# First stage of a two-stage kernel: PE's small products behind convolution products, weights of two images mixed one phase later, norms applied by ScalarE

## Chip, cores and metric

The kernel runs on one core of a Trainium2 chip. The metric is the device time of one execution in microseconds (us), the median of several runs.

## What is computed

A batch of 32 images of 32x32 pixels and 64 channels passes two residual layers, each behind a group norm (32 groups of two channels). The first one is what this case is about:

```python
for t in range(3):                                   # STEPS
    k, v = x @ Wk, x @ Wv                            # two heads of 16
    attn = softmax(q . k / 4 over the 1024 pixels)
    logits = pooled(attn, v) @ Wmlp                  # one number for each of 4 experts
    weights = softmax(where(allowed, logits, -1e9) / 1.5)
    wsel = the two largest weights, normalized to sum 1
    x_mod = x * (1 + mean_over_heads(attn) * 1024 * softplus(alpha))
    x = sum over e of wsel[e] * (conv3x3(x_mod, We[e]) + be[e])
    allowed loses the top expert of this step (never the last one)
x_out = x_in + x                                     # then the second group norm
```

The second layer is two Mamba scans, over rows and over columns. The change does not touch it.

## The kernel before

`stage1` (L243) computes the first layer and both group norms, `stage2` (L873) the scans. Stage 1 keeps an image as 128 partitions (two row parities x 64 channels) by 512 pixels. Four images are a team, two teams a body, four bodies the batch. For each body there are six phases k = 0 to 5: step k // 2 of team g = k % 2. So while the vector work of a phase decides on the weights of one team, TensorE runs the convolution of the other team, which is the phase before (`last` in `slot`, L511). The convolution is not done four times, once for each expert: VectorE mixes the four experts' weights with `wsel` first (`mix_first`, `mix_second`, `mix_last`, L821 to L836; ScalarE's `scale_experts` makes the first term), and TensorE multiplies once, by six fp32 products of 128x512 for each image: three on the padded image (`conv_main`, L495) and three on a copy shifted by a row (`conv_anti`, L504, the copy is ScalarE's `shift`).

Each engine has an order written out by hand, its `slot`, and meets the others by counting semaphores; nothing is scheduled by a program. For phase P the chain between the engines is: `score` (PE, L459, four products into `p_route`) -> `reduce_max` (DVE, L736) -> `swap` (PE, L465) -> `neg_top` (DVE, L743) -> `exp` (ACT, L596) -> the weighted sum `parts` (DVE, L755) -> `total` (PE, L469) -> `r`, `ratio`, `ratios`, `kmap`, `mod_w` (DVE, L760 to L765) -> `logits` (PE, L473) and `modulation` (PE, L479) -> the choice of experts, `wsel` (DVE, L782 to L811) with ScalarE's `prob` in it -> `scale_experts` and the mixes. `modulate` (DVE, L776) writes the padded image. ScalarE's `step_out` (L570) moves a finished convolution to `xc`, from which `score` of the next step of that team reads; in the last step DVE's `step_last` (L701) adds it to `x1` instead.

Group norms are laid into some phases (`norm_in_phase`, L371): the input norm of team 0 in k = 5 and of team 1 in k = 0, the norm of the result of team 0 in k = 1 and of team 1 in k = 2. That makes 4 of 6 phases of a body "norm phases" (in the first body only k = 0). Each has `norm_moments` (DVE, L652, four `bn_stats`), two tiny products on PE (`group_mean` L441, `group_var` L446), `norm_variance_in`, `norm_variance`, ScalarE's Ln and Exp (`group_root`) and `norm_apply` (DVE, L674), whose last increment (`x_norm` or `x_out`) lets `score` or the stores of the SP queue go on. A hardware loop (`each_phase`, L358) runs k = 5 of a body with k = 0 to 4 of the next, three times.

Of the kernel before, what the change touches and what calls it, by code (L numbers as in the profile page):

```python
# [24 lines left out]
PHASES = 2 * STEPS  # L25
# [222 lines left out]
def stage1(nc, x_in, mid_x, norm_rows, c):  # L248
# [10 lines left out]
    with ctx:  # L259
# [61 lines left out]
        gn_rs = sem("s1_gn_rs")  # L321
        x_norm = sem("s1_x_norm")
# [115 lines left out]
        def _(pe):  # L438
# [69 lines left out]
            def slot(i, k, before, after):  # L508
                norm = norm_in_phase(i, k, before, after)
                P = i * PHASES + k  # L510
                last = (i, k - 1) if k else (i - 1, PHASES - 1)  # L511
                runs_conv = k > 0 or before
                if runs_conv:
                    conv_main(*last, 0)
                score(i, k, TEAM - 1)
                swap(P)
                if norm:
                    group_mean(norm[0])
                if runs_conv:
                    conv_anti(*last, 0)  # L520
                total(P)
                if norm:
                    group_var(norm[0])
                if runs_conv:
                    conv_main(*last, 1)
                logits(P)
                modulation(P, 0)
                modulation(P, 1)
                if runs_conv:
                    conv_anti(*last, 1)  # L530
                    conv_main(*last, 2)
                modulation(P, 2)
                if runs_conv:
                    conv_anti(*last, 2)
                modulation(P, 3)
                if runs_conv:
                    conv_main(*last, 3)
                    conv_anti(*last, 3)
                if after:
                    for a in range(TEAM - 1):  # L540
                        score(*((i, k + 1) if k < PHASES - 1 else (i + 1, 0)), a)
# [17 lines left out]
        def _(act):  # L559
            def group_root(n):  # L560

                act.wait_ge(gn_v, n + 1)
                nc.scalar.activation(gn[:, 4, :], gn[:, 3, :], ACT.Ln).then_inc(gn_ln, 1)
                act.wait_ge(gn_ln, n + 1)
                nc.scalar.activation(gn[:, 5, :], gn[:, 4, :], ACT.Exp, scale=-0.5).then_inc(gn_rs, 1)

# [53 lines left out]
            group_root(0)  # L620
            act.wait_ge(zeroed, ZEROS)
            each_phase(act, slot)
            group_root(4 * BODIES - 2)
            group_root(4 * BODIES - 1)

# [10 lines left out]
        def _(dve):  # L636
# [25 lines left out]
            def norm_variance_in(n):  # L662

                dve.wait_ge(gn_mean, n + 1)
                chain(nc.vector.tensor_copy(gn[:, 0, :], p_gn[:, P_MEAN]))
# [8 lines left out]
            def norm_apply(n, src, dst, finish):  # L674
# [7 lines left out]
                for a in team:  # L682
                    to = dst[a][:] if finish is x_norm else dst[a][:, :, PAD:]
                    x = src[a][:] if finish is x_norm else src[a][:].rearrange("p (j w) -> p j w", w=SIDE)
# [4 lines left out]
            def group_norm(n, src, dst, finish):  # L689
                norm_moments(src)  # L690
                norm_variance_in(n)
                norm_variance(n)
                norm_apply(n, src, dst, finish)
# [13 lines left out]

            def slot(i, k, before, after):
                g, t = k % 2, k // 2
                P = i * PHASES + k  # L710
                if k == PHASES - 1 and not isinstance(i, int):
# [8 lines left out]
                if norm:  # L720
                    number, kind, pair = norm
                    body = i + 1 if k == PHASES - 1 else i
                    src, dst, finish = ((fresh[pair], xc[pair], x_norm) if kind == "in" else
                                        (x1[pair], xn[pair], x_out))
# [26 lines left out]
                if norm:  # L751
                    norm_variance_in(number)
# [15 lines left out]
                if norm:  # L768
                    norm_variance(number)
# [50 lines left out]

                def mix_first(a):  # L821
                    dve.wait_ge(scaled, 4 * P + a + 1)
                    nc.vector.scalar_tensor_tensor(mix0[a % 2][:], c["we"][:, 1, :], wsel[:, a, 1:2], mix0[a % 2][:],  # L823
                                                   ALU.mult, ALU.add).then_inc(mix_ready, 1)

                def mix_second(a):
                    dve.wait_ge(mix_ready, 8 * P + (1, 2, 5, 6)[a])
                    nc.vector.scalar_tensor_tensor(mix0[a % 2][:], c["we"][:, 2, :], wsel[:, a, 2:3], mix0[a % 2][:],
                                                   ALU.mult, ALU.add).then_inc(mix_ready, 1)

                def mix_last(a):
                    dve.wait_ge(mix_ready, 8 * P + (3, 4, 7, 8)[a])

                    ge(dve, conv_done, 4 * (P - 2) + a + 1)
                    nc.vector.scalar_tensor_tensor(w_mixed[g][a][:].rearrange("p m d c -> p (m d c)"), c["we"][:, 3, :],
                                                   wsel[:, a, 3:4], mix0[a % 2][:], ALU.mult, ALU.add).then_inc(w_ready, 1)  # L836
# [16 lines left out]
                if norm and kind == "out":  # L853
                    norm_apply(number, src, dst, finish)
# [9 lines left out]
            group_norm(0, fresh[0], xc[0], x_norm)  # L864
            each_phase(dve, slot)
            x1_last = (BODIES - 1, 1)
            group_norm(4 * BODIES - 2, x1[0], xn[0], x_out)
            step_last(*x1_last, team)
            x1_complete(*x1_last)
            group_norm(4 * BODIES - 1, x1[1], xn[1], x_out)  # L870
# [637 lines left out]
```

## Time and profile before

| | us |
|---|---|
| median of 3 runs | 4278.47 (4276.27 to 4280.89) |
| the profiled execution, its own time | 4277.8 |
| its span in the trace | 4275.8 |
| busy in the span: PE | 3856.6 (90%) |
| DVE | 3902.4 (91%) |
| ACT | 2860.6 (67%) |
| POOL | 3142.5 (73%) |

Stage 1 runs from 31.6 to 932 us of the span, stage 2 from there to the end. PE's granted clock over the whole execution has a mean of 0.952 of full speed. A "busy" PE may still run at half clock, and "idle before" is the time that an engine stood in front of an instruction, with what ended it.

### The profile page before, as it was taken

The numbers are of one execution on the slowest core, as the hardware profiler recorded it, in microseconds if no ns is written. First come the engines' busy times: TensorE is split into PE (matmuls) and PEld (weight loads), VectorE is DVE, ScalarE is ACT, GpSimd is POOL, SyncE is SP. The second block draws the span as 40 slices with busy tenths as digits, with TensorE's granted clock in tenths as the row PEclk, the third lists the DMA queues.
The fourth block names the chain that finished last, engine by engine and source line by source line (L and its number), as shares of the span: only waits on it lengthen the run. The fifth ranks groups of instructions, "written<-read, shape, count | busy, mean of one in ns | idle before, by whom it ended". The sixth has DMA issues, their size and how long they took to land. (4 is left out here: it accounts for less than half of the span.)

```text
span 4275.8 us, 49280 instructions
## 1 busy us (share of the span) xinstructions
PE 3856.6 (90%) x8924; PEld 1606.4 (38%) x8924; DVE 3902.4 (91%) x5354; ACT 2860.6 (67%) x4337; POOL 3142.5 (73%) x1446
## 2 busy tenths in 40 slices
PE   4988988869999999999999999999999999999998
PEld 2333333323333333333333333333333333333433
DVE  5676767659999999999999999999999999999998
ACT  2323232327777777777777777777777777777775
POOL 0000000009999999999999999999999999999998
PEclk8999999989999999999999999999999999999999
DMA  2001010128888888888888888888888888888886
GB/s 74 0 23 59 20 61 0 61 104 350 330 342 342 345 328 340 345 331 337 328 345 342 344 342 325 337 339 349 341 320 348 343 338 329 329 342 345 349 337 256
DMA packets 199056, 1156.59 MB, mean 270 GB/s; under 512 B 30001, under 2 KB 30801, under 8 KB 67665
## 3 DMA queue, kind: packets, MB, share of 16 engines
q1 hardware_dynamic: 198736, 1153.31, 68.9%
q14 instruction: 239, 1.95, 0.1%
q8 instruction: 81, 1.33, 0.1%
HBM read 1118.87 MB, written 34.34 MB: 270 GB/s over the span
## 5 line engine op out<-in xcount | busy, mean ns | idle before, releaser
L1362 POOL TENSOR_TENSOR read<-state,bc_all 128x1024 f32<-128x1024 f32 x1024 | 2401.8, 2362 | 182.2 <-DVE state L1420 170.7
L1420 DVE TENSOR_TENSOR_SCAN state<-decays,p_drive 128x512 f32<-128x512 f32 x2048 | 2430.1, 1207 | 38.3 <-ACT decays L1297 18.4
L1148 PE MATMUL p_y<-read,ident 128*128 128x512 f32 x4096 | 1998.7, 622 | 26.1 <-issue 17.1
L1297 ACT ACTIVATE decays<-dt,wa 128x496 f32<-128x496 f32 x2048 | 1322.3, 698 | 19.3 <-issue 16.9
L1148 PEld LDWEIGHTS p_y<-read,ident 128*128 128x128 f32 x4096 | 793.1, 198 | 1064.7 <-issue 950.7
L1409 DVE TENSOR_TENSOR p_drive<-bc_all,p_dtx 128x512 f32<-128x512 f32 x1536 | 1037.5, 675 | 0.0
L1369 POOL TENSOR_TENSOR dtx<-dt,xconv 128x512 f32<-128x512 f32 x128 | 163.5, 1278 | 916.5 <-ACT dt L1244 916.5
L1379 POOL TENSOR_TENSOR pool_drive<-dtx,bc_all 128x1024 f32<-128x1024 f32 x256 | 603.8, 2359 | 0.9 <-DMA bc_all<-bc_scratch 0.9
L1305 ACT COPY p_drive<-pool_drive 128x1024 f32<-128x1024 f32 x256 | 259.7, 1014 | 325.2 <-POOL pool_drive L1379 325.2
L1144 PE MATMUL p_y<-xconv,d_diag 128*128 128x512 f32 x256 | 161.7, 716 | 207.9 <-DVE gated L1428 207.9
L504 PE MATMUL p_conv<-shf,wm 128*128 128x512 f32 x576 | 303.9, 669 | 0.0
L1244 ACT COPY dt<-p_b 128x512 f32<-128x512 f32 x128 | 75.0, 586 | 303.7 <-PE p_b L1139 303.7
L495 PE MATMUL p_conv<-pad,wm 128*128 128x512 f32 x576 | 269.9, 605 | 0.0
L570 ACT ACTIVATE xc<-p_conv,bias 128x512 f32<-128x512 f32 x64 | 44.0, 687 | 210.9 <-PE p_conv L504 210.9
L1223 ACT ACT_TABLE_LOAD x128 | 164.2, 1283 | 22.8 <-PE p_a L1096 20.5
L823 DVE SCALAR_TENSOR_TENSOR mix<-we_sb,wsel,mix 128x768 f32<-128x768 f32 x96 | 94.9, 1016 | 91.2 <-ACT mix L577 91.0
L504 PEld LDWEIGHTS p_conv<-shf,wm 128*128 128x128 f32 x576 | 115.7, 211 | 156.6 <-issue 152.0
L1232 ACT ACT_TABLE_LOAD x128 | 164.2, 1283 | 2.3
L1102 PE MATMUL p_a<-cols_in,w_cols 128*128 128x256 f32 x640 | 157.2, 394 | 3.9 <-ACT cols_in L1290 3.9
L1144 PEld LDWEIGHTS p_y<-xconv,d_diag 128*128 128x128 f32 x256 | 39.8, 195 | 314.1 <-DVE gated L1428 313.0
L495 PEld LDWEIGHTS p_conv<-pad,wm 128*128 128x128 f32 x576 | 106.3, 191 | 134.5 <-issue 121.6
L1124 PE MATMUL p_a<-xconv,wbc 128*32 128x512 f32 x256 | 134.7, 608 | 15.3 <-ACT xconv L1223 14.8
(164 smaller groups left out, 3316.5 us busy)
## 6 DMA issues: line engine op xcount, KB each, us to landing
bc_all<-bc_scratch SPq DMA_DIRECT2D x1024, 1024.0 KB, 7.2
norm_rows<-xn SPq DMA_DIRECT2D x32, 280.0 KB, 2.8
norm_in<-norm_rows SPq DMA_DIRECT2D x64, 140.0 KB, 6.0
norm_in<-norm_rows SPq DMA_DIRECT2D x64, 139.8 KB, 7.1
fresh<-in_x SPq DMA_DIRECT2D x32, 256.0 KB, 3.3
x<-in_x SPq DMA_DIRECT2D x32, 256.0 KB, 3.5
mid_x<-x SPq DMA_DIRECT2D x32, 256.0 KB, 2.6
resid<-mid_x SPq DMA_DIRECT2D x32, 256.0 KB, 7.6
```

The source lines that it names most:

```text
L495: nc.tensor.matmul(bank[:], w_mixed[g][a][:, 0, dx, :], padded[g][a][:, :, dx:dx + SIDE], start=(dx == 0), stop=False)
L504: mm = nc.tensor.matmul(bank[:], w_mixed[g][a][:, 1, dx, :], shifted[g][a][:, :, dx:dx + SIDE], start=False, stop=(dx == 2))
L1144: nc.tensor.matmul(p_y[:], d_diag[unit[0]][:], xconv[b][:], start=True, stop=False).then_inc(skip_added, 1)
L1148: nc.tensor.matmul(p_y[:], ident[:], read[:, s % DEEP, :], start=False, stop=(s == N - 1)).then_inc(y_added, 1)
L1223: nc.scalar.activation(same_shape(xconv[b][:], m), in_order(p_a, m), ACT.Silu, bias=wcb[m][:]).then_inc(xconv_ready, 1)
L1232: nc.scalar.preload_act_table_set("natural_log_exp_and_others")
L1297: nc.scalar.activation(decays[s % DEEP][:].rearrange("p (q t) -> p q t", t=SIDE)[:, :, 1:], dt[b][:, :, 1:], ACT.Exp, scale=wa[m][:, s:s + ...
L1305: nc.scalar.copy(p_drive[:, s % 4:s % 4 + 2, :], pool_drive[n][:]).then_inc(drive_moved, 1)
L1362: nc.gpsimd.tensor_tensor(read[:, s % DEEP:s % DEEP + 2, :], state[:, s % DEEP:s % DEEP + 2, :], bc_all[:, s:s + 2, 1, :], ALU.mult).then_ ...
L1379: nc.gpsimd.tensor_tensor(pool_drive[n][:], dtx[b][:].unsqueeze(1).broadcast_to([128, 2, PIX]), bc_all[:, s:s + 2, 0, :], ALU.mult).then_i ...
L1409: nc.vector.tensor_tensor(p_drive[:, s % 4, :], bc_all[:, s, 0, :], p_dtx[:], ALU.mult).then_inc(drive_done, 1)
L1420: nc.vector.tensor_tensor_scan(state[:, s % DEEP, :], decays[s % DEEP][:], p_drive[:, s % 4, :], 0.0, ALU.mult, ALU.add).then_inc(scan_don ...
```

## The change

1. PE's `slot`: `swap` (and `group_mean`) now stand behind `conv_anti(last, 0)`, `total` and `group_var` behind `conv_main(last, 1)`, and `logits` and the first two modulations behind `conv_anti(last, 1)`; the later ones are shifted by half an image likewise.
2. DVE: of images 2 and 3 the six mixes are no longer done at the end of their own phase but in the next one (`late`): two behind `reduce_max`, two behind `parts`, one behind `ratios` (and `norm_variance`), one behind `mod_w`. For the last phase of all they stand in front of the closing norms.
3. DVE: `norm_moments` stands in front of `reduce_max` instead of behind it.
4. `norm_apply` moves from DVE to ScalarE (four `activation` with scale and bias for each norm). DVE computes the bias -mean x rstd by one more small instruction (`norm_scale`), earlier than before: in front of the mixes of images 0 and 1. DVE waits (`free`) until the norm before has been applied before it overwrites `gn`.
5. ScalarE: `group_root` in front of `prob`; `norm_apply` behind `scale_experts` 0 and 1; both shifts of images 0 and 1 in front of `scale_experts` 2 and 3.

The diff, cut:

```diff
@@ PE slot
                 score(i, k, TEAM - 1)
+                if runs_conv:
+                    conv_anti(*last, 0)
                 swap(P)
                 if norm:
                     group_mean(norm[0])
                 if runs_conv:
-                    conv_anti(*last, 0)
+                    conv_main(*last, 1)
                 total(P)
                 if norm:
                     group_var(norm[0])
                 if runs_conv:
-                    conv_main(*last, 1)
+                    conv_anti(*last, 1)
                 logits(P)
                 modulation(P, 0)
                 modulation(P, 1)
                 if runs_conv:
-                    conv_anti(*last, 1)
                     conv_main(*last, 2)
+                    conv_anti(*last, 2)
                 modulation(P, 2)
                 if runs_conv:
-                    conv_anti(*last, 2)
+                    conv_main(*last, 3)
                 modulation(P, 3)
                 if runs_conv:
-                    conv_main(*last, 3)
                     conv_anti(*last, 3)
@@ ScalarE
+            def norm_apply(n, kind, pair):
+                act.wait_ge(gn_scale, n + 1)
+                for a in team:
+                    src, dst = ((fresh[pair][a][:], xc[pair][a][:]) if kind == "in" else
+                                (x1[pair][a][:].rearrange("p (j w) -> p j w", w=SIDE), xn[pair][a][:, :, PAD:]))
+                    o = nc.scalar.activation(dst, src, ACT.Identity, scale=gn[:, 9, a:a + 1], bias=gn[:, 7, a:a + 1])
+                o.then_inc(x_norm if kind == "in" else x_out, 1)
@@ ScalarE slot
+                if norm:
+                    group_root(norm[0])
                 act.wait_ge(wexp_in, P + 1)
                 nc.scalar.activation(prob[:], logit[:], ACT.Exp, scale=1.0 / 1.5).then_inc(wexp_done, 1)
-                if norm:
-                    group_root(norm[0])
...
                 scale_experts(P, 0)
                 scale_experts(P, 1)
+                if norm:
+                    norm_apply(*norm)
                 if steps:
                     step_out(i, k - 1, 2)
                 shift(P, g, 0)
+                shift(P, g, 1)
                 scale_experts(P, 2)
-                shift(P, g, 1)
+                scale_experts(P, 3)
                 if steps:
                     step_out(i, k - 1, 3)
-                scale_experts(P, 3)
                 shift(P, g, 2)
                 shift(P, g, 3)
@@ DVE: norm_apply becomes norm_scale
-                for a in team:
...
-                    o = nc.vector.tensor_scalar(to, x, gn[:, 0, a:a + 1], gn[:, 9, a:a + 1],
-                                                ALU.subtract, ALU.mult)
-                o.then_inc(finish, 1)
+                nc.vector.scalar_tensor_tensor(gn[:, 7, :], gn[:, 0, :], -1.0, gn[:, 9, :],
+                                               ALU.mult, ALU.mult).then_inc(gn_scale, 1)
@@ DVE slot
+                def late(stage, *images):
+
+                    if runs_conv:
+                        for a in images:
+                            stage(P - 1, 1 - g, a)
...
+                    free = {5: (x_out, 2 * i), 0: (x_norm, 2 * i + 1), 1: (x_norm, 2 * i + 2), 2: (x_out, 2 * i - 1)}[k]
...
-                dve.wait_ge(score_done, P + 1)
-                nc.vector.reduce_max(top[0:R, :], p_route[0:R, :], X).then_inc(top_ready, 1)
                 if norm:
                     if kind == "in":
                         dve.wait_ge(fresh_in[pair], 16 * TEAM * body + 16 * TEAM)
                     norm_moments(src)
+                dve.wait_ge(score_done, P + 1)
+                nc.vector.reduce_max(top[0:R, :], p_route[0:R, :], X).then_inc(top_ready, 1)
+                late(mix_first, 2, 3)
...
+                late(mix_second, 2, 3)
                 dve.wait_ge(sum_done, P + 1)
...
+                if norm:
+                    norm_variance(number)
+                late(mix_last, 2)
                 chain(nc.vector.tensor_scalar(kmap[:], r[:], float(PIX), c["gain"][0:R, 3:4], ALU.mult, ALU.mult))
...
-                if norm:
-                    norm_variance(number)
+                late(mix_last, 3)
...
+                if norm:
+                    norm_scale(number)
                 for stage in (mix_first, mix_second, mix_last):
                     for a in (0, 1):
-                        stage(a)
+                        stage(P, g, a)
                 modulate(2)
-                if norm and kind == "in":
-
-                    norm_apply(number, src, dst, finish)
                 modulate(3)
-                for stage in (mix_first, mix_second, mix_last):
-                    for a in (2, 3):
-                        stage(a)
@@ DVE, behind the last phase
             each_phase(dve, slot)
             x1_last = (BODIES - 1, 1)
+            for stage in (mix_first, mix_second, mix_last):
+                for a in (2, 3):
+                    stage(PHASES * BODIES - 1, 1, a)
```

How the order moves. First TensorE, from `score` of image 3 of a phase without a norm (k = 2 of the first body) to its third modulation. Before:

```order
L459 MATMUL p_route<-xc,route 128x512
L465 MATMUL p_small<-top,neg_swap 128x1
L504 MATMUL p_conv<-shf,wm 128x512 x3
L469 MATMUL p_small<-parts,both_par 128x2
L495 MATMUL p_conv<-pad,wm 128x512 x3
L473 MATMUL p_small<-ratios,ones 128x16
L479 MATMUL p_modul<-attn,mod_w 128x512 x2
L504 MATMUL p_conv<-shf,wm 128x512 x3
L495 MATMUL p_conv<-pad,wm 128x512 x3
L479 MATMUL p_modul<-attn,mod_w 128x512
```

The same stretch after the change:

```order
L460 MATMUL p_route<-xc,route 128x512
L505 MATMUL p_conv<-shf,wm 128x512 x3
L466 MATMUL p_small<-top,neg_swap 128x1
L496 MATMUL p_conv<-pad,wm 128x512 x3
L470 MATMUL p_small<-parts,both_par 128x2
L505 MATMUL p_conv<-shf,wm 128x512 x3
L474 MATMUL p_small<-ratios,ones 128x16
L480 MATMUL p_modul<-attn,mod_w 128x512 x2
L496 MATMUL p_conv<-pad,wm 128x512 x3
L505 MATMUL p_conv<-shf,wm 128x512 x3
```

Three convolution products stand between `score` and `swap` now, where none did; three between `swap` and `total` and three between `total` and `logits`, as before.

Then VectorE in the same phase, from `reduce_max` (`top`) to `mod_w`. Before (the six mixes of images 2 and 3 stood just ahead of this):

```order
L736 TENSOR_REDUCE top<-p_route 64x1
L743 SCALAR_TENSOR_TENSOR neg_top<-top,p_small 64x1
L748 SCALAR_TENSOR_TENSOR allowed<-rank,allowed 128x4x3
L750 TENSOR_SCALAR penalty<-allowed 128x16
L755 ISA scrap,parts<-p_route,attn 64x512
L755 ISA parts 64x1
L760 RECIPROCAL r<-p_small 64x1
L761 TENSOR_TENSOR ratio<-p_small,r 64x1
L762 TENSOR_SCALAR ratios<-pick,ratio 64x16
L763 TENSOR_SCALAR kmap<-r,gain 64x1
L765 TENSOR_SCALAR mod_w<-spread,kmap 64x512
```

After the change, from `neg_top` on (ahead of it stand `top` and, new, two mixes `mix_0` and `mix_1` of images 2 and 3):

```order
L783 SCALAR_TENSOR_TENSOR neg_top<-top,p_small 64x1
L788 SCALAR_TENSOR_TENSOR allowed<-rank,allowed 128x4x3
L790 TENSOR_SCALAR penalty<-allowed 128x16
L795 ISA scrap,parts<-p_route,attn 64x512
L795 ISA parts 64x1
L728 SCALAR_TENSOR_TENSOR mix_0<-we_sb,wsel,mix_0 128x768
L728 SCALAR_TENSOR_TENSOR mix_1<-we_sb,wsel,mix_1 128x768
L801 RECIPROCAL r<-p_small 64x1
L802 TENSOR_TENSOR ratio<-p_small,r 64x1
L803 TENSOR_SCALAR ratios<-pick,ratio 64x16
L735 SCALAR_TENSOR_TENSOR wm<-we_sb,wsel,mix_0 128x768
L807 TENSOR_SCALAR kmap<-r,gain 64x1
```

Five of the six moved mixes now stand inside the chain from `top` to `mod_w`, two of them between `parts` and `r`.

## Rows read from the trace of the kernel before

**Rows 1.** Windows: length, busy PE, PEld, DVE, ACT, POOL, then clock, DMA share, GB/s.
```profile
46.26:84.16 37.90, 23.74 (x40) 9.89 (x40) 26.23 (x74) 9.51 (x17) 0.00 (x0) 0.68 0.16 55
84.16:206.30 122.14, 118.31 (x280) 48.78 (x280) 80.03 (x184) 46.94 (x76) 0.00 (x0) 1.00 0.00 0
206.30:858.02 651.72, 578.25 (x1308) 243.24 (x1308) 454.05 (x1165) 199.72 (x342) 0.00 (x0) 0.92 0.10 37
858.02:932.26 74.24, 49.44 (x112) 21.55 (x112) 39.15 (x105) 10.04 (x19) 0.00 (x0) 0.82 0.16 60
```

**Rows 2.** The same view by phase: a plain one, k = 0, 1, 2, 3.
```profile
145.24:175.77 30.53, 29.58 (x70) 12.20 (x70) 20.00 (x47) 11.73 (x19) 0.00 (x0) 1.00 0.00 1
...
678.17:715.39 37.22, 33.16 (x74) 14.03 (x74) 28.98 (x76) 9.52 (x17) 0.00 (x0) 0.91 0.00 0
715.39:755.49 40.10, 33.31 (x74) 14.19 (x74) 26.59 (x72) 12.04 (x21) 0.00 (x0) 0.91 0.00 0
755.49:794.33 38.84, 32.26 (x74) 13.77 (x74) 26.58 (x73) 12.03 (x21) 0.00 (x0) 0.90 0.23 84
794.33:827.49 33.16, 32.20 (x70) 13.35 (x70) 20.09 (x48) 11.73 (x19) 0.00 (x0) 0.91 0.27 98
```

**Rows 3.** Timeline of PE around one plain phase's start (start, duration, engine, line).
```profile
607.79 1.02 PE L459 MATMUL p_route<-xc,route 128*128 128x512 f32 x2
...
609.76 0.38 PE L465 MATMUL p_small<-top,neg_swap 128*128 128x1 f32 x2 [0.95 <-DVE top L736]
610.01 2.82 PE L504 MATMUL p_conv<-shf,wm 128*128 128x512 f32 x6
...
612.67 0.28 PE L469 MATMUL p_small<-parts,both_par 128*128 128x2 f32 x2
612.81 2.82 PE L495 MATMUL p_conv<-pad,wm 128*128 128x512 f32 x6
...
615.56 0.39 PE L473 MATMUL p_small<-ratios,ones 64*128 64x16 f32 x2
615.80 1.96 PE L479 MATMUL p_modul<-attn,mod_w 64*128 64x512 f32 x4
```

**Rows 4.** The same timeline: DVE and ACT of that phase.
```profile
609.04 0.67 DVE L736 TENSOR_REDUCE top<-p_route 64x1 f32<-64x512 f32 x1
...
610.19 0.15 DVE L743 SCALAR_TENSOR_TENSOR neg_top<-top,p_small 64x1 f32<-64x1 f32 x1 [0.47 <-PE p_small L465]
...
611.37 0.69 DVE L755 CUSTOM_DVE_ANT_0 scrap<-p_route,attn 64x512 f32<-64x512 f32 x1 [0.74 <-ACT attn L596]
...
612.99 0.16 DVE L760 RECIPROCAL r<-p_small 64x1 f32<-64x1 f32 x1 [0.92 <-PE p_small L469]
...
613.36 0.23 DVE L762 TENSOR_SCALAR ratios<-pick,ratio 64x16 f32<-64x16 f32 x1
...
613.84 0.48 DVE L765 TENSOR_SCALAR mod_w<-spread,kmap 64x512 f32<-64x512 f32 x1
```

**Rows 5.** Timeline of a norm phase (k = 0): PE, then DVE.
```profile
681.70 0.59 PE L441 MATMUL p_gn<-moments,group_mean 128*128 128x4 f32 x2 [2.41 <-DVE moments L659]
682.15 5.47 PE L504 MATMUL p_conv<-shf,wm 128*128 128x512 f32 x6
...
678.78 2.46 DVE L654 BATCH_NORM_STATS2 stats<-fresh 128x6 f32<-128x512 f32 x4
...
704.11 0.15 DVE L678 TENSOR_TENSOR gn<-gn 128x4 f32<-128x4 f32 x1
...
705.70 1.92 DVE L685 TENSOR_SCALAR xc<-fresh,gn 128x512 f32<-128x512 f32 x4
...
708.13 1.94 DVE L823 SCALAR_TENSOR_TENSOR mix<-we_sb,wsel,mix 128x768 f32<-128x768 f32 x2
709.98 1.94 DVE L828 SCALAR_TENSOR_TENSOR mix<-we_sb,wsel,mix 128x768 f32<-128x768 f32 x2
```

**Rows 6.** Group of ScalarE's instructions, 40 to 930 us: busy, mean ns, idle before.
```profile
L570 ACT ACTIVATE xc<-p_conv,bias 128x512 f32<-128x512 f32 x64 | 44.0, 687 | 210.9 <-PE p_conv L504 210.9
```

More of the change, by code:

```diff
@@ L321, in stage1 @@
         gn_rs = sem("s1_gn_rs")
+        gn_scale = sem("s1_gn_scale")
         x_norm = sem("s1_x_norm")
@@ L620, in _ @@
             group_root(0)
+            norm_apply(0, "in", 0)
             act.wait_ge(zeroed, ZEROS)
@@ L623, in _ @@
             group_root(4 * BODIES - 2)
+            norm_apply(4 * BODIES - 2, "out", 0)
             group_root(4 * BODIES - 1)
+            norm_apply(4 * BODIES - 1, "out", 1)
         @block.gpsimd
@@ L660, in norm_moments, with norm_variance_in @@
                 ag.then_inc(gn_mean_in, 1)
-            def norm_variance_in(n):
+            def norm_variance_in(n, free=None):
                 dve.wait_ge(gn_mean, n + 1)
+                if free:
+                    ge(dve, *free)
                 chain(nc.vector.tensor_copy(gn[:, 0, :], p_gn[:, P_MEAN]))
@@ L672, in norm_variance, with norm_scale @@
                 nc.vector.tensor_scalar(gn[:, 3, :], p_gn[:, P_VAR], 1e-5, None, ALU.add).then_inc(gn_v, 1)
-            def norm_apply(n, src, dst, finish):
+            def norm_scale(n):
                 dve.wait_ge(gn_rs, n + 1)
@@ L681, in norm_apply, with group_norm @@
                     chain(nc.vector.tensor_tensor(gn[:, dst_r, :], gn[:, 6, :], gn[:, src_r, :], ALU.mult))
-                for a in team:
-                    to = dst[a][:] if finish is x_norm else dst[a][:, :, PAD:]
-                    x = src[a][:] if finish is x_norm else src[a][:].rearrange("p (j w) -> p j w", w=SIDE)
-                    o = nc.vector.tensor_scalar(to, x, gn[:, 0, a:a + 1], gn[:, 9, a:a + 1],
-                                                ALU.subtract, ALU.mult)
-                o.then_inc(finish, 1)
-            def group_norm(n, src, dst, finish):
+                nc.vector.scalar_tensor_tensor(gn[:, 7, :], gn[:, 0, :], -1.0, gn[:, 9, :],
+                                               ALU.mult, ALU.mult).then_inc(gn_scale, 1)
+            def group_norm(n, src, free=None):
                 norm_moments(src)
-                norm_variance_in(n)
+                norm_variance_in(n, free)
                 norm_variance(n)
-                norm_apply(n, src, dst, finish)
+                norm_scale(n)
             def step_last(i, g, some):
@@ L706, in x1_complete, with mix_first, mix_second, mix_last @@
                 dve.wait_ge(x1_ready, 8 * i + 4 * g + 4)
+            def mix_first(P, g, a):
+                dve.wait_ge(scaled, 4 * P + a + 1)
+                nc.vector.scalar_tensor_tensor(mix0[a % 2][:], c["we"][:, 1, :], wsel[:, a, 1:2], mix0[a % 2][:],
+                                               ALU.mult, ALU.add).then_inc(mix_ready, 1)
+            def mix_second(P, g, a):
+                dve.wait_ge(mix_ready, 8 * P + (1, 2, 5, 6)[a])
+                nc.vector.scalar_tensor_tensor(mix0[a % 2][:], c["we"][:, 2, :], wsel[:, a, 2:3], mix0[a % 2][:],
+                                               ALU.mult, ALU.add).then_inc(mix_ready, 1)
+            def mix_last(P, g, a):
+                dve.wait_ge(mix_ready, 8 * P + (3, 4, 7, 8)[a])
+                ge(dve, conv_done, 4 * (P - 2) + a + 1)
+                nc.vector.scalar_tensor_tensor(w_mixed[g][a][:].rearrange("p m d c -> p (m d c)"), c["we"][:, 3, :],
+                                               wsel[:, a, 3:4], mix0[a % 2][:], ALU.mult, ALU.add).then_inc(w_ready, 1)
             def slot(i, k, before, after):
@@ L710, in slot @@
                 P = i * PHASES + k
+                runs_conv = k > 0 or before
+                def late(stage, *images):
+                    if runs_conv:
+                        for a in images:
+                            stage(P - 1, 1 - g, a)
                 if k == PHASES - 1 and not isinstance(i, int):
@@ L722, in slot @@
                     body = i + 1 if k == PHASES - 1 else i
-                    src, dst, finish = ((fresh[pair], xc[pair], x_norm) if kind == "in" else
-                                        (x1[pair], xn[pair], x_out))
+                    src = fresh[pair] if kind == "in" else x1[pair]
+                    free = {5: (x_out, 2 * i), 0: (x_norm, 2 * i + 1), 1: (x_norm, 2 * i + 2), 2: (x_out, 2 * i - 1)}[k]
                 if k == PHASES - 1:
@@ L751, in slot @@
                 if norm:
-                    norm_variance_in(number)
+                    norm_variance_in(number, free)
                 dve.wait_ge(exp_done, P + 1)
@@ L819, in slot @@
                 chain(nc.vector.reduce_sum(bias[g][:], bias_e[:], X))
[L821 to L836, printed above, removed]
+                if norm:
+                    norm_scale(number)
                 for stage in (mix_first, mix_second, mix_last):
                     for a in (0, 1):
-                        stage(a)
+                        stage(P, g, a)
                 modulate(2)
-                if norm and kind == "in":
-                    norm_apply(number, src, dst, finish)
                 modulate(3)
-                for stage in (mix_first, mix_second, mix_last):
-                    for a in (2, 3):
-                        stage(a)
                 if ending:
@@ L852, in slot @@
                     x1_complete(*ending)
-                if norm and kind == "out":
-                    norm_apply(number, src, dst, finish)
             loop_start = [0]
@@ L863, in _ @@
             dve.wait_ge(fresh_in[0], 16 * TEAM)
-            group_norm(0, fresh[0], xc[0], x_norm)
+            group_norm(0, fresh[0])
             each_phase(dve, slot)
             x1_last = (BODIES - 1, 1)
-            group_norm(4 * BODIES - 2, x1[0], xn[0], x_out)
+            for stage in (mix_first, mix_second, mix_last):
+                for a in (2, 3):
+                    stage(PHASES * BODIES - 1, 1, a)
+            group_norm(4 * BODIES - 2, x1[0], (x_out, 2 * BODIES - 2))
             step_last(*x1_last, team)
             x1_complete(*x1_last)
-            group_norm(4 * BODIES - 1, x1[1], xn[1], x_out)
+            group_norm(4 * BODIES - 1, x1[1], (x_out, 2 * BODIES - 1))
 def stage2(nc, mid_x, norm_rows, out, c):
```

## Prediction

> **What bounds the kernel now.** I read the windows first, by stretch, and see where stage 1's time lies: the first phase takes 37.90 us (with the first `score`, which starts at 46.3), four phases without a norm 122.14, the 18 phases of the three loop turns 651.72, and the last phase with the close 74.24 [rows 1]. Stage 2 is not touched, so only these 886 of 4276 us can move, but for 932.26 us minus 46.26 nothing else runs beside them. Then the windows by phase [rows 2]. A plain phase lasts 30.53 us with PE busy 29.58 at a granted clock of 1.00: PE bounds it. Norm phases last 37.22 (k = 0), 40.10 (k = 1) and 38.84 (k = 2), with k = 5 measured like k = 0, and the clock falls to 0.91. There PE waits, and VectorE, though busy only 26.6 to 29.0 of about 38 us, is what it waits for: VectorE's 28.98 in k = 0 all lie ahead of the next `top`, but for a wait in the middle.
>
> The timeline says where PE loses time. In a plain phase it stands still 0.95 us between `score` and `swap`, since `top` must be made first; nothing is queued that could fill it [rows 3]. In a norm phase it waits 2.41 us more in front of `group_mean`, because four `bn_stats` (2.46 us) stand between `top` and the moments, and the convolution products that come next last from 682.15 to the next product at 687.41, 5.26 us instead of the 2.66 of a plain phase (610.01 to 612.67) [rows 3, 5]: TensorE runs them at 1.2 instead of 2.4 GHz after that stand. The rest is VectorE's end of the phase: six mixes, and ahead of or behind them eight small instructions (704.11 to 705.70) and four applications (1.92 us) [rows 5].
>
> **The change, part by part.** Call A the moment at which PE is through with `score` of image 3. A product is issued every 0.86 us (its row ends 0.16 later than the next one can start), so in the plain phase A = 607.79 + 0.86 = 608.65 [rows 3].
>
> *PE's floor.* A phase holds the same products before and after. A plain one without any stand takes 30.53 - 0.95 - 0.16 = 29.42 us. A norm phase has two tiny products more, 0.45 us for one on its own (681.70 to 682.15 [rows 5]) and about 0.3 in a stream like `total` and `logits` (0.14 and 0.24 [rows 3]): floor 30.0.
>
> *The chain from A to the first modulation, plain phase.* PE: `conv_anti` 0 takes 2.57, `swap` 0.25, `conv_main` 1 2.67, `total` 0.14, `conv_anti` 1 2.77, `logits` 0.24: PE could start the modulations at A + 8.64. VectorE: `top` starts at A + 0.27 (0.39 in the row, where VectorE was 0.12 late) and takes 0.61 to the next start; two late mixes at 0.93 each (1.85 for a pair [rows 5]) end at A + 2.75, which `swap` (A + 2.57) covers. `neg_top` starts 0.43 behind `swap`, at A + 3.00; `parts` starts 1.18 later (610.19 to 611.37 [rows 4]), A + 4.18, and takes 0.69. PE's `total` waits for `parts` no longer than PE is busy (A + 5.49). Now two mixes, to A + 6.73; without them `r` would have started 0.32 behind `total`, at A + 5.81, so they cost 0.9. `ratios` starts 0.37 later and takes 0.15 to the next start, A + 7.25; one mix, A + 8.18; `kmap` and `mod_w` (0.33 + 0.48 [rows 4]) end at A + 8.99. PE takes the modulations about 0.05 later, at A + 9.04: a stand of 0.4 us where PE could have gone on at 8.64. Period 29.42 + 0.4 = 29.8, against 30.53. The moved `swap` saves 1.1 us, the mixes in the chain give back 0.4.
>
> *Does VectorE reach the next `top` in time?* From `mod_w` on: one mix, `logits` 0.73, `modulate` and the choice of experts to `wsel` (about 3.4 with the first modulate), A + 13.8; `bias` and ScalarE's first terms, A + 16.3; six mixes 5.6, two modulates 1.2: A + 23.1. The next `top` is due at A + 30.1, so 7 us are free.
>
> *Norm phases.* PE runs 0.5 us later by its tiny products, VectorE 0.2 later by `norm_variance`; the four small instructions of `norm_variance_in` lie beside ScalarE's exp. So the stand nearly closes: period 30.0 to 30.1. VectorE carries `norm_scale` (nine at 0.20 = 1.8), the moments (2.8 with `bn_aggr`), in k = 5 and 0 four `step_last` (2.8) and with k = 0 and 1 behind it two memsets: 23.1 + 0.2 + 1.8 + 2.8 + 2.8 + 0.2 = A + 30.9 less the 0.4 that the sum of a plain phase waits for ScalarE and I count twice, about A + 30.5, against 30.3. On time to some tenths, and `swap` needs `top` only 2.57 behind A, so up to a microsecond is free. ScalarE: `norm_apply` starts at about A + 18.5 and takes 4 x 0.6 = 2.5 (0.687 each [rows 6], starts 0.6 apart), so `x_norm` is there at A + 21.1; the next `score` needs it at A + 24.8. In k = 1 and 2 `step_out` 2 stands behind it and is done at A + 21, needed at 26.5. ScalarE has room (9.5 to 12.0 us busy in such a phase [rows 2]). PE has no stand of microseconds left, so nothing runs at 1.2 GHz; that is worth 2.6 us in each of k = 0, 1, 2, 3, and part of k = 5.
>
> *First phase.* `x_norm` 0 comes 0.8 later, by ScalarE's slower application and one instruction. Then the moments leave the way from `top` to `neg_top` (-2.3, since `swap` still takes 0.5), six mixes and a modulate leave the way to `x_norm` 1 (-5.8 and -0.6 with what they stood behind), application and handover cost 1.0 more: 0.8 - 2.3 - 6.4 + 1.0 = -6.9.
>
> *Close.* VectorE has the six own late mixes (5.6) behind the last phase, in which it also did those of the phase before. They stood there before too, but `step_last` and the modulates now wait for PE until A + 24.8, then six mixes end at A + 30.4; before, the moments began at 885.5, 27.9 behind A. All of PE's last products wait for these: +2.5. The last application on ScalarE +1.0. Together +3.5.
>
> *Sum.* First phase -6.9; four plain phases 4 x 29.8 = 119.2 against 122.14, -2.9; 18 looped ones 3 x (4 x 30.05 + 2 x 29.8) = 539.4 against 651.72, -112.3; close +3.5. That is -118.6 against the profiled execution's 4277.8: 4159.2. Its time is 0.7 under the median of the runs, so 4160 for the median.
>
> A rule speaks against the move to ScalarE. Here an application costs 1.92 / 4 = 0.48 us on VectorE [rows 5] and 0.6 to 0.69 on ScalarE [rows 6]. The Trainium skill ("ScalarE: Activation LUTs", Rules for kernel authors) says to use VectorE and not ScalarE for multiplications and additions, and budgets some 0.3 us plus 0.83 ns per element for an activation, 0.73 us here; the trace agrees in the direction. By it each norm would take 1.0 us longer, which counts only in the first phase and the close: the sum would stand within a microsecond of mine.
>
> **Rivals.**
> (a) *VectorE's chain is longer than I count*, by semaphore latencies between the late mixes and their neighbours, 0.5 to 1.2 us a phase. For it: `mod_w` is late already in my sum, so each tenth goes straight into all 22 phases. Against: most handovers are read from rows. 22 x 0.5 to 1.2 = 11 to 26: 4171 to 4186. Chance 0.14.
> (b) *The floor is reached*: `mod_w` is in time. 4 x 0.4 + 6 x 0.4, some tenths in the norm phases, and less at the close: 4150 to 4154. Chance 0.06.
> (c) *Norm phases stay bound by VectorE*: its sum in k = 5 and 0 comes within tenths of the period. If it is 2 us longer there, six or seven phases lose 1 to 2 beyond the slack, and with k = 1 as many: 4175 to 4195. Chance 0.05.
> (d) *The rule above decides*: ScalarE waits for `norm_scale`, and `scale_experts` and `step_out` wait behind it. It decides when `x_norm` is over 3.7 us later than counted; each microsecond beyond costs one in six phases. Applications at 0.73 bring 0.5, so they don't. With 2 us beyond, 4172. Chance 0.02.
> (e) *Slower than before.* In the chain from `parts` to `mod_w` a late mix waits for an event of PE that itself stands behind the modulation, so that PE stands until VectorE is through with its queue. Nearest case: VectorE reaching `mod_w` only where it now reaches the first mixes of a phase, some 7 us later. It decides from 118.6 / 22 = 5.4 us a phase; at 7 it would be 4160 + 154 = 4314. Against: `mix_last` waits for convolutions two phases back and for its own predecessors alone. Chance 0.01.
> (f) *The change does nothing*, PE's products being issued so far ahead that order does not matter. The 0.95 us in front of `swap` in every plain phase speak against. 4278, chance 0.01.
> A slower-than-before outcome short of (e), by anything else, gets 0.01.
>
> **How the numbers follow.** My forecast, 4155 to 4168, has 0.70. The range takes in (b) and most of (a), and half of (c): 4150 to 4180. About 0.2% (8.6 us) can be told from no change: 0.97 faster, 0.01 the same, 0.02 slower.
>
> **What would show it.** The windows: plain phases of 29.8 us, norm phases of 30.0 to 30.2, clock 1.00 from the first body to the last phase. The timeline of PE: no stand in front of `swap`, `group_mean` or `total`, one of about 0.4 in front of the first modulation of a plain phase, `conv_anti` 0 in 2.6 us everywhere. VectorE idle some 7 us in front of `top` in plain phases and almost nothing in k = 0 and 1. It is wrong if PE waits for `mod_w` more than a microsecond (a), for `x_norm` (d), or for `top` (c).

## The result and the profile after

The changed kernel takes 4160.77 us (median of 4 runs, 4157.54 to 4161.57) against 4279.15: a ratio of 0.9722, 95% interval 0.9708 to 0.9737, 118 us less. Its profiled span is 4159.5 us. The forecast was 4160.

The windows of the changed kernel, cut at its own starts of `top`, the first from 46.26 as in [rows 1] (columns as there): first phase, four plain phases, 18 looped ones.

```profile
46.26:76.70 30.44, 22.58 (x41) 9.20 (x42) 16.99 (x61) 13.44 (x23) 0.00 (x0) 0.78 0.22 69
76.70:195.13 118.43, 117.84 (x281) 49.39 (x280) 82.04 (x193) 47.31 (x76) 0.00 (x0) 1.00 0.00 0
195.13:736.53 541.40, 535.91 (x1309) 227.65 (x1308) 429.86 (x1119) 235.46 (x390) 0.00 (x0) 1.00 0.12 44
```

Beside [rows 1], the first phase gave 37.90 - 30.44 = 7.5 us, the plain phases 3.7 and the 18 looped ones 110.3. The close, from the last `top` to the first memset of stage 2, grew from 74.2 to 77.0 (736.53 to 813.57). What is left to the 116.3 us between the spans lies in stage 2, which was 2.4 us longer in this execution, with the same code.

The same view by phase: a plain one of the first body, then k = 5, 0, 1, 2 and the plain k = 3 of the loop.

```profile
135.88:165.50 29.62, 29.48 (x71) 12.35 (x70) 19.82 (x46) 11.83 (x19) 0.00 (x0) 1.00 0.00 1
...
556.07:586.34 30.27, 29.93 (x75) 12.79 (x74) 27.42 (x74) 12.56 (x21) 0.00 (x0) 1.00 0.00 0
586.34:616.35 30.01, 29.92 (x75) 12.80 (x74) 27.33 (x73) 12.56 (x21) 0.00 (x0) 1.00 0.00 0
616.35:646.54 30.19, 29.92 (x75) 12.80 (x74) 24.77 (x69) 14.86 (x25) 0.00 (x0) 1.00 0.26 94
646.54:676.73 30.19, 29.93 (x75) 12.80 (x74) 21.99 (x60) 14.86 (x25) 0.00 (x0) 1.00 0.29 107
676.73:706.63 29.90, 29.47 (x71) 12.35 (x70) 19.94 (x46) 11.83 (x19) 0.00 (x0) 1.00 0.04 14
```

These answer to [rows 2], where the norm phases took 37.2, 40.1 and 38.8. All phases are now within 0.7 us of each other, PE is busy in nearly all of each, and its clock is 1.00. VectorE's busy time fell little in k = 0 (28.98 to 27.33, the applications less `norm_scale`): the rest of its work moved to where it had been idle.

PE and VectorE at the start of a looped plain phase, from the timeline.

```profile
525.97 2.74 PE L505 MATMUL p_conv<-shf,wm 128*128 128x512 f32 x6
526.17 0.68 DVE L779 TENSOR_REDUCE top<-p_route 64x1 f32<-64x512 f32 x1 [8.09 <-PE p_route L460]
526.78 1.93 DVE L723 SCALAR_TENSOR_TENSOR mix<-we_sb,wsel,mix 128x768 f32<-128x768 f32 x2
528.54 0.28 PE L466 MATMUL p_small<-top,neg_swap 128*128 128x1 f32 x2
...
528.86 0.15 DVE L783 SCALAR_TENSOR_TENSOR neg_top<-top,p_small 64x1 f32<-64x1 f32 x1 [0.15 <-PE p_small L466]
...
531.34 0.28 PE L470 MATMUL p_small<-parts,both_par 128*128 128x2 f32 x2
...
533.17 1.02 DVE L735 SCALAR_TENSOR_TENSOR wm<-we_sb,wsel,mix 128x768 f32<-128x768 f32 x1
534.11 0.20 DVE L807 TENSOR_SCALAR kmap<-r,gain 64x1 f32<-64x1 f32 x1
534.23 0.39 PE L474 MATMUL p_small<-ratios,ones 64*128 64x16 f32 x2
534.44 0.48 DVE L809 TENSOR_SCALAR mod_w<-spread,kmap 64x512 f32<-64x512 f32 x1
...
535.05 1.12 PE L480 MATMUL p_modul<-attn,mod_w 64*128 64x512 f32 x2 [0.42 <-DVE mod_w L809]
```

With A = 525.97, `swap` and `total` start without a stand, where [rows 3] has 0.95 us in front of `swap`. The one stand left is 0.42 us in front of the first modulation, for `mod_w`. VectorE was idle 8.09 us before `top`. In the norm phases too PE has no stand in front of `swap`, `group_mean` or `total`, and 0.27 to 0.35 us in front of the first modulation in k = 5, 1 and 2.

### The profile page after: what moved, and what is told of

Read it like the earlier page. It is cut to its first block and busy times, and to the rows that moved or that the text cites. A ratio compares the mean times of both kernels' runs of the same rounds, so it can differ in the third digit from the quotient of the medians.

```text
span 4159.5 us, 49327 instructions
## 1 busy us (share of the span) xinstructions
PE 3808.2 (92%) x8924; PEld 1590.0 (38%) x8924; DVE 3872.5 (93%) x5306; ACT 2908.2 (70%) x4401; POOL 3142.3 (76%) x1446
## 5 line engine op out<-in xcount | busy, mean ns | idle before, releaser
L505 PE MATMUL p_conv<-shf,wm 128*128 128x512 f32 x576 | 267.2, 600 | 0.0
L505 PEld LDWEIGHTS p_conv<-shf,wm 128*128 128x128 f32 x576 | 105.4, 189 | 133.7 <-issue 133.7
L1125 PEld LDWEIGHTS p_a<-cols_in,w_cols 128*128 128x128 f32 x640 | 127.6, 200 | 56.8 <-issue 31.9
L1155 PE MATMUL p_b<-xconv,wdt 128*128 128x512 f32 x256 | 144.9, 648 | 0.0
```

What stands on the lines that cost most here:

```text
L505: mm = nc.tensor.matmul(bank[:], w_mixed[g][a][:, 1, dx, :], shifted[g][a][:, :, dx:dx + SIDE], start=False, stop=(dx == 2))
L1125: mm = nc.tensor.matmul(p_a[:, 256 * p:256 * p + 256], w_cols[:, n, :], cols_in[:, HALF * half:HALF * half + HALF, 2 - shift:2 - shift + R ...
```

## The experiments

I take four parts of the changed kernel: PE's order, the late mixes, the moments in front of `top`, the applications on ScalarE. Each was undone alone, and PE's order was also made alone. ScalarE's own new order (point 5 of the change) was undone in no run, so what it is worth is not known. My theory: VectorE's queue is what bound the norm phases, and PE's order makes the room in which VectorE can be late. The main rival: PE's order carries the gain by itself.

**PE's order alone.** PE's `slot` of the changed kernel in the kernel before:

```diff
                 score(i, k, TEAM - 1)
+                if runs_conv:
+                    conv_anti(*last, 0)
                 swap(P)
...
                 if runs_conv:
-                    conv_anti(*last, 0)
+                    conv_main(*last, 1)
                 total(P)
...
```

> The kernel before with PE's new order alone. Theory (the gain comes from VectorE's relief, PE's order only makes room for it): plain phases fall from 30.5 to 29.4, since nothing stands in front of swap any more; norm phases stay bound by VectorE, whose work is unchanged, at 33 to 36 us; about 50 us less than before, 4215 to 4240. Rival (PE's order carries the gain, by the hidden swap and the end of the half-clock products): norm phases near 31, 4160 to 4180.

Measured: 4222.96 us, ratio 0.9863 (0.9846 to 0.9879), inside the theory's range and far from the rival's. Its windows, a plain phase and k = 5, 0, 1, 2:

```profile
145.13:174.45 29.32, 29.32 (x71) 12.28 (x70) 20.02 (x48) 11.62 (x19) 0.00 (x0) 1.00 0.00 1
408.01:442.54 34.53, 30.13 (x75) 12.67 (x74) 28.98 (x76) 9.51 (x17) 0.00 (x0) 1.00 0.08 31
442.54:476.79 34.25, 30.18 (x75) 12.72 (x74) 28.98 (x76) 9.52 (x17) 0.00 (x0) 1.00 0.09 31
476.79:511.20 34.41, 31.05 (x77) 12.99 (x75) 26.60 (x73) 11.93 (x21) 0.00 (x0) 1.00 0.00 0
511.20:548.09 36.89, 32.68 (x74) 13.83 (x74) 26.59 (x74) 11.92 (x21) 0.00 (x0) 0.91 0.23 88
```

The plain phase is PE through and through, 29.32 busy of 29.32. The norm phases of this turn fall from 37 to 40 us to 34 to 37 and stay VectorE's, whose 28.98 us of work are what they were. Even so PE's order alone brings 57.6 us (4280.51 - 4222.96), nearly half of the whole: 49.0 of them in the 18 looped phases (651.72 to 602.70), where PE's busy time for the same products fell by 23.1 (578.25 to 555.15), mostly as fewer ran slowly. The theory called it only the room for the rest; it is more than that.

**PE's order undone.** The changed kernel with PE's old `slot`, the diff above turned round.

> The changed kernel with PE's old order. Theory (the late mixes need three convolution products in front of swap): PE stands about 1.1 us in front of swap, 0.7 in front of total and 0.95 in front of the first modulation; plain phases 32.0, norm phases 32.5, so some 50 us more than the changed kernel, 4200 to 4220, and plain phases slower than before's 30.5. Rival (the order of PE is worth only the 1.1 us in front of swap): 22 x 1.1 = 24, 4180 to 4190.

Measured: 4232.18, 71 more than the changed kernel, ratio to the kernel before 0.9889 (0.9872 to 0.9905). PE in a plain phase of the first body, then in one of the loop:

```profile
173.64 0.38 PE L466 MATMUL p_small<-top,neg_swap 128*128 128x1 f32 x2 [0.78 <-DVE top L778]
...
177.22 0.38 PE L470 MATMUL p_small<-parts,both_par 128*128 128x2 f32 x2 [0.51 <-DVE parts L794]
...
181.27 1.98 PE L480 MATMUL p_modul<-attn,mod_w 64*128 64x512 f32 x4 [0.67 <-DVE mod_w L808]
...
384.04 1.98 PE L480 MATMUL p_modul<-attn,mod_w 64*128 64x512 f32 x4 [0.88 <-DVE mod_w L808]
385.94 4.54 PE L505 MATMUL p_conv<-shf,wm 128*128 128x512 f32 x6
390.32 2.74 PE L496 MATMUL p_conv<-pad,wm 128*128 128x512 f32 x6
```

The three stands are where they were expected, if shorter (0.78, 0.51 and 0.67 us), and the plain phase takes 31.97 us, 1.4 more than before the change: in plain phases the late mixes cost without PE's new order. Taken together, VectorE's and ScalarE's changes still bring 48.3 us without it (4280.51 - 4232.18). With the 57.6 of PE's order alone that is 106 of the 118 us; the other 12 come only when both are there. The total lies 12 us above the expected range, and the last rows show why: products that take 4.38 us (385.94 to 390.32) instead of the 2.67 of the next three. The last section tells more of it.

**Late mixes undone.** `late` removed, all mixes in their own phase:

```diff
...
                 modulate(2)
                 modulate(3)
+                for stage in (mix_first, mix_second, mix_last):
+                    for a in (2, 3):
+                        stage(P, g, a)
```

> The changed kernel with all mixes of images 2 and 3 in their own phase. Theory: plain phases 29.4 (VectorE has 7 to 8 us free there, and mod_w is early, so the stand of PE goes); norm phases k = 5 and 0 are bound by VectorE, about 33 to 34 us against 30.1, k = 1 and k = 2 32 and 30.5; the close 2 to 3 us shorter. 20 us more in all, 4170 to 4190. Rival (the late mixes only cost, as they stand in the chain): below 4155.

Measured: 4175.83, ratio 0.9755 (0.9739 to 0.9772), 15 more. Plain phase, k = 5, 0, 1, 2:

```profile
137.03:166.34 29.31, 29.31 (x71) 12.28 (x70) 20.00 (x47) 11.76 (x19) 0.00 (x0) 1.00 0.00 1
384.60:417.44 32.84, 30.73 (x76) 12.64 (x74) 27.32 (x76) 12.55 (x21) 0.00 (x0) 1.00 0.09 32
417.44:451.73 34.29, 31.71 (x74) 13.38 (x74) 27.31 (x76) 12.56 (x21) 0.00 (x0) 0.95 0.09 31
451.73:483.36 31.63, 30.93 (x73) 13.24 (x74) 24.84 (x72) 14.87 (x25) 0.00 (x0) 0.95 0.29 101
483.36:511.55 28.19, 28.19 (x71) 11.89 (x70) 22.15 (x62) 14.95 (x25) 0.00 (x0) 1.00 0.29 104
```

Plain phases gain (29.31 against 29.62 and 29.90), norm phases lose, k = 0 most. Part of that loss is the clock: k = 0 takes 34.29 us in this turn at a clock of 0.95, and 32.61 in the third turn at 1.00. k = 2 looks short only because `top` at its start was late and at its end was not; PE had gone on.

**Moments undone.** `norm_moments` behind `reduce_max` again.

> The changed kernel with norm_moments behind reduce_max again. Theory: in each of 13 norm phases 2.8 us come between top and neg_top; PE stands about 2.5 us in front of total or the first modulation; 13 x 2.5 = 33 more, 4185 to 4200; plain phases unchanged at 29.6 to 29.9. Rival (the late mixes or PE's products cover it as they cover the mixes): within 5 us of the changed kernel.

Measured: 4197.77, ratio 0.9805 (0.9788 to 0.9821), 37 more, with plain phases unchanged at 29.91. k = 5 and k = 0:

```profile
395.82:431.94 36.12, 33.75 (x75) 13.88 (x74) 27.31 (x74) 12.56 (x21) 0.00 (x0) 0.91 0.09 29
431.94:464.31 32.37, 30.35 (x75) 12.80 (x74) 27.04 (x73) 12.56 (x21) 0.00 (x0) 1.00 0.10 33
```

k = 0 grew by 2.4 us, about as expected; where the clock fell besides, as in this k = 5 (0.91), 3.4 us of slower products come on top. Six of the 12 looped norm phases have such products, 11.8 us of the 41.6 by which the looped phases grew together. Of the four parts but PE's order this is the largest, and it is a move of 2.8 us of work past one instruction.

**Applications back on VectorE.** ScalarE's `norm_apply` goes, and the last lines of `norm_scale` are again:

```diff
...
+                for a in team:
+                    src, dst = ((fresh[pair][a][:], xc[pair][a][:]) if kind == "in" else
+                                (x1[pair][a][:].rearrange("p (j w) -> p j w", w=SIDE), xn[pair][a][:, :, PAD:]))
+                    o = nc.vector.tensor_scalar(dst, src, gn[:, 0, a:a + 1], gn[:, 9, a:a + 1],
+                                                ALU.subtract, ALU.mult)
...
```

> The changed kernel with the four applications of a norm on VectorE, where norm_scale stands. Theory: 1.9 us more on VectorE less the one small instruction, 1.7; VectorE had 0.63 and 0.81 us free in front of top at the ends of k = 5 and k = 0 and 2.6 to 8.1 elsewhere, so only these two grow, by about 0.9 us each: 3 x 1.8 = 5.4 more; the first phase and the close get 1 us shorter each. About 3 us more than the changed kernel, 4158 to 4167: the move to ScalarE is worth almost nothing. Rival (the move is a main part of the gain, 1.7 us in each of 13 norm phases): 22 more, 4180 or above.

Measured: 4159.41, ratio 0.9725 (0.9712 to 0.9738): no difference from the changed kernel that can be told. k = 5 and k = 0:

```profile
376.39:407.32 30.93, 30.93 (x77) 13.19 (x76) 29.01 (x76) 9.73 (x17) 0.00 (x0) 1.00 0.11 34
407.32:437.76 30.44, 29.75 (x75) 12.73 (x74) 28.81 (x78) 9.73 (x17) 0.00 (x0) 1.00 0.10 35
```

They grow by 0.7 and 0.4, and k = 1 shrinks by 0.3: 543.85 us for the 18 looped phases against 541.40. Stage 1 ends 1.9 us later (815.49 against 813.57), less than the runs can tell, and about what was expected.

**Both reliefs of VectorE undone.** The last two edits together.

> The changed kernel with all mixes in their own phase and the applications on VectorE: both reliefs of VectorE's queue undone at once. With the mixes alone undone it took 4176, with the applications alone 4159, that is 15 and about 0 more than the changed kernel. Theory (the two unload the same queue, so that the second is worth nothing only while the first is there): VectorE sets the norm phases k = 5, 0 and 1, each grows by up to 1.7 us, and k = 3, which catches up, no longer can everywhere: 10 to 20 more than with the mixes alone, 4185 to 4197. Rival (the effects add): 15 more than the changed kernel, 4173 to 4178.

Measured: 4197.99, ratio 0.9807 (0.9794 to 0.982). The late mixes undone cost 15 us with the applications on ScalarE and 39 with them on VectorE (4197.99 - 4159.41); the applications cost 22 us (4197.99 - 4175.83) where the mixes are not late, and nothing where they are. The two do not add; they are two ways to empty one queue. The rival is refuted, and the size was 1 us above my range.

**The last stand: `mod_w` first.**

```diff
-                late(mix_last, 2)
                 chain(nc.vector.tensor_scalar(kmap[:], r[:], float(PIX), c["gain"][0:R, 3:4], ALU.mult, ALU.mult))
...
-                late(mix_last, 3)
+                late(mix_last, 2, 3)
```

> The changed kernel with the late mix_last of image 2 behind mod_w. Theory (the last stand of PE is mod_w's, by one 0.93 us mix too many in front of it): the stand goes; plain phases fall to 29.3, norm phases to 29.8; in all 0.3 x 4 + 0.6 x 6 + 0.37 x 12 = 9 us less, 4148 to 4154. Rival (PE's products are the whole of the period and the stand lies beside something else): no change, 4160.

Measured: 4148.25, ratio 0.9696 (0.9683 to 0.9709), 12.5 less than the changed kernel. The four plain phases, the 18 looped ones, and k = 5:

```profile
78.46:195.63 117.17, 117.17 (x281) 49.11 (x280) 81.68 (x193) 47.34 (x76) 0.00 (x0) 1.00 0.00 1
195.63:728.61 532.98, 532.98 (x1309) 226.36 (x1308) 429.45 (x1120) 235.54 (x390) 0.00 (x0) 1.00 0.13 45
...
373.29:403.05 29.76, 29.76 (x75) 12.73 (x74) 27.34 (x73) 12.56 (x21) 0.00 (x0) 1.00 0.10 36
```

PE is busy for the whole of both stretches, and every phase has its floor: 29.31 or 29.76. 541.40 - 532.98 = 8.4 and 118.43 - 117.17 = 1.3 are what the stands in front of the modulation were worth; the other 2.8 us of the 12.5 are within the scatter of the runs.

**Late mixes only behind norm phases.** On top of `mod_w` first:

```diff
-                    if runs_conv:
+                    if {0: before, 1: True, 2: before, 3: before}.get(k, False):
...
                 modulate(3)
+                if not norm:
+                    for stage in (mix_first, mix_second, mix_last):
+                        for a in (2, 3):
+                            stage(P, g, a)
```

> The kernel with mod_w ahead of the late mixes, and besides late mixes only for norm phases; plain phases and the very last one do all six in their own phase. Theory: VectorE has 7 to 8 us free at the end of plain phases, so no phase grows; plain phases 29.3; the close 2.5 us shorter. About 2 us less than with mod_w first alone, 4145 to 4152. Rival (the moments of k = 5 behind the six own mixes of k = 4 come too late): k = 4 or 5 is 1 to 2 us longer in each turn, 4152 to 4158.

Measured: 4147.9, ratio 0.9702 (0.9689 to 0.9715), the same as without this edit: the phases were at their floor already, and 2 us of the close are less than the runs tell. The rival shows as a late `top` at the start of k = 5 (k = 4 seems 30.85 to 31.01 us long, k = 5 28.2), which costs nothing, as `swap` stands behind three products.

**The close.** On top of both edits before, PE lays the closing norm of team 0 between the last convolutions, VectorE two `step_last` in front of its wait for it:

```diff
-            group_mean(4 * BODIES - 2)
-            group_var(4 * BODIES - 2)
             for a in team:
                 conv_main(BODIES - 1, PHASES - 1, a)
+                if a == 2:
+                    group_var(4 * BODIES - 2)
                 conv_anti(BODIES - 1, PHASES - 1, a)
+                if a == 1:
+                    group_mean(4 * BODIES - 2)
...
```

> The kernel before this one in the list, with the closing norm of team 0 laid between the last convolution products (group_mean behind image 1, group_var between the two halves of image 2) instead of in front of them. Theory: PE stands 6 to 9 us there and then runs at half clock; both go, the last convolution ends 11 to 13 us earlier and so does stage 1: 4133 to 4141. Rival (the close is set by the stores of team 0 or by the start of stage 2): less than 5 us.

Measured: 4133.99 (4133.51 to 4138.57), ratio 0.9666 (0.9653 to 0.9679): the best of all, 27 us under the changed kernel and 144 under the kernel before. The timeline of PE in the close, first of the changed kernel:

```profile
769.43 0.59 PE L442 MATMUL p_gn<-moments,group_mean 128*128 128x4 f32 x2 [9.42 <-DVE moments L674]
...
771.31 4.78 PE L496 MATMUL p_conv<-pad,wm 128*128 128x512 f32 x6
775.92 2.74 PE L505 MATMUL p_conv<-shf,wm 128*128 128x512 f32 x6
```

then of this version:

```profile
752.43 2.74 PE L496 MATMUL p_conv<-pad,wm 128*128 128x512 f32 x6
755.01 2.74 PE L505 MATMUL p_conv<-shf,wm 128*128 128x512 f32 x6
...
762.87 0.28 PE L442 MATMUL p_gn<-moments,group_mean 128*128 128x4 f32 x2
763.01 2.82 PE L496 MATMUL p_conv<-pad,wm 128*128 128x512 f32 x6
```

The stand of 9.42 us, which held no work that PE needed, is gone, and the slower products behind it too (4.78 us for three, against 2.74). Without this edit, but with the two before it, the stand was 8.55 us. Stage 1 ends 12.0 us earlier than without this edit (793.12 against 805.08).

## Why the prediction was right

The mechanism held, as the windows, the timeline and the runs above show. The forecast was 0.8 us off, closer than its terms, and that is luck: they missed by 0.6 to 2 us and cancelled.

*Plain phases, forecast 29.8.* 29.62 us in the first body, 29.90 in the loop. The chain came as counted, with the stand in front of the modulation in its place. The floor I took from rows was 29.42; it is 29.31.

*Norm phases, forecast 30.0 to 30.1.* 30.27, 30.01, 30.19, 30.19, with a floor of 29.76 where I had 30.0: I took 0.3 us for each tiny product though my rows gave 0.14 and 0.24, and two of them add 0.45 (29.76 - 29.31). The stand there did not close as I thought. The loop came to 541.4 against 539.4.

*VectorE in time for `top`.* At the end of k = 5 it waited 0.63 us for `score`, at the end of k = 0 0.81; I had it 0.2 late. The step was right in kind: these are the tight places, and the two phases that grew when its work grew by 1.7 us.

```profile
225.39 0.68 DVE L779 TENSOR_REDUCE top<-p_route 64x1 f32<-64x512 f32 x1 [0.63 <-PE p_route L460]
255.40 0.68 DVE L779 TENSOR_REDUCE top<-p_route 64x1 f32<-64x512 f32 x1 [0.81 <-PE p_route L460]
```

*Clock.* 1.00 from the second phase to the last `top`, as forecast; in the first phase it was 0.78, and it fell again at the stand of 9.42 us in the close. It is a large part of the gain: for the same products PE's busy time in the 18 looped phases fell by 42.3 us (578.25 in [rows 1] to 535.91), over a third of the 110.3. My 2.6 us in each of four phases of a turn, 31 us, and a part for k = 5 agree with that. Rival (b), the floor, did not come by this change, but one moved mix makes it real, at 4148 where I had put 4150 to 4154. Rivals (a), (c) and (d) did not occur; (c) is what the run with both reliefs undone shows. The rival that ends on the slower side (e) did not occur either, nor did (f), no change at all.

*First phase and close.* -7.5 against -6.9, and +2.8 against +3.5. The first `score` started 0.9 us later than before (47.20 against 46.31), where I had 0.8. But with the applications back on VectorE the first phase ended at 76.67, against 76.70 of the changed kernel, so the 1.0 us that I charged to them at its end does not show. In the close VectorE began the moments 30.2 us behind A (766.49 - 736.34), not 30.4. Counted from the last `top`, PE's last product ended 1.6 us later than before (57.57 against 55.93), where I had 2.5, and the last application 2.6 later (68.57 against 65.93), so ScalarE's 1.0 came as counted.

*ScalarE's application.* I took 0.6 us each from the copies of `step_out` [rows 6]. They take 0.80 and start 0.71 apart:

```profile
L574 ACT ACTIVATE xc<-fresh,gn 128x512 f32<-128x512 f32 x32 | 23.4, 802 | 16.8 <-DVE gn L699 16.8
```

`step_out` reads PSUM with a bias only, the application reads SBUF with a scale and a bias; which of the two makes the difference was not tried. The estimate of 0.73 by the Trainium skill ("ScalarE: Activation LUTs", Rules for kernel authors) was nearer than my rows. Its advice against ScalarE for such work was right by the price, and the run with the applications on VectorE shows that the move brought nothing here; but with the mixes in their own phase it is worth 22 us. The price of one instruction says nothing on which queue is full.

## What to carry to other kernels

When an engine is busy for only two thirds to four fifths of a phase and yet bounds it, look for where in the order it is idle and move work there, and put long products of the waiting engine between each question and its answer. Here each move alone brought less than half of the whole (57.6 and 48.3 of 118 us), and the mixes moved without room for them made the plain phases longer. The parts of such a change don't add: undo each alone, and two together, before calling one useless. And after it, look at what is left in front of the first waiting instruction; one mix too many in front of `mod_w` was worth 10 us in 22 phases.

## What was not expected of the hardware

*The clock also fell where all stands were short.* With PE's old order and the late mixes, PE stands three times within some 10 us of a phase: 0.78, 0.59 and 0.88 us in a looped plain phase, and nowhere in the looped phases longer than the 1.09 us of k = 5. In 11 phases one after the other, from k = 5 of the first turn to k = 3 of the second, three products took 4.38 us instead of 2.67, and a phase lasted 33.9 to 34.3 us at a clock of 0.95. In the seven looped phases behind them, with the same stands (0.78, 0.59 and 0.87 in the plain ones, 1.09 in k = 5), and in the plain phases of the first body (0.78, 0.51 and 0.67), the clock stayed at 1.00. The two rows are k = 3 and k = 4 of the second turn, on either side of the turning point.

```profile
545.93:579.88 33.95, 31.71 (x70) 12.77 (x70) 19.85 (x47) 11.84 (x19) 0.00 (x0) 0.95 0.00 0
579.88:612.12 32.24, 30.01 (x70) 12.18 (x70) 22.69 (x55) 11.84 (x19) 0.00 (x0) 1.00 0.00 1
```

That is 11 phases at 1.7 us, 19 us, and without these 19 us that run would lie in its range, at about 4213. What decides between the one and the other was not settled.

*The same phase is slower inside the hardware loop, where VectorE's chain bounds it.* A plain phase takes 29.90 us there against 29.62; with `mod_w` first it is 29.31 in both places. `mod_w` begins 0.24 us behind `kmap` in the first body and 0.33 in the loop, and the first modulation comes 8.80 and 9.08 us behind A. As far as the code of these instructions goes, only the waits differ, which compare with a register's value in the loop and with a constant outside. That this is the cause is only argued; no run has tried it.
